# Decoder layer on one core: column scales multiplied into the float32 FFN weights, one VectorE operation per FFN row tile, and an earlier release for GpSimd

## What is computed

```python
x = layernorm(x + mamba(x))                 # conv, selective scan over 1024 x 16 states, out projection
x = layernorm(x + cross_attention(x, ctx))  # softmax(q k^T), used as x @ attention^T
x = layernorm(x + ffn(x))

def ffn(x, weight, bias):                   # int8 in effect: both sides rounded to -127..127
    w_scale = max(|weight|, axis=1) / 127   # one per output column o
    w_q = round(weight / w_scale)
    x_scale = max(|x|, axis=2) / 127        # one per row
    x_q = round(x / x_scale)
    return (x_q @ w_q.T) * x_scale * w_scale[o] + bias
```

## Time and profile before

| | us |
|---|---|
| median of 3 runs | 1086.15 (1085.72 to 4713.28) |
| the profiled execution, its own time | 1085.01 |
| its span (first to last instruction) | 1083.1 |

### The profile page before, as it was taken

The page is one execution under the profiler, slowest core; times in us unless marked ns, Lnnn a source line. Parts: engine busy times, 40 slices in busy tenths (PEclk is TensorE's granted clock), DMA queues, the critical chain, the costliest instruction groups (busy, mean ns, idle before and its releaser), DMA issues.

```text
span 1083.1 us, 10459 instructions
## 1 busy us (share of the span) xinstructions
PE 850.6 (79%) x2958; PEld 334.8 (31%) x2968; DVE 1017.7 (94%) x861; ACT 790.7 (73%) x1171; POOL 667.3 (62%) x260
## 2 busy tenths in 40 slices
PE   8945788786799899687599899887699475755985
PEld 3321233231233344232134344332133132222432
DVE  3699999999999998999999998999999999999746
ACT  4486687776766898997766898998676695876524
POOL 1056666666676766776667756786766766776343
PEclk9987798898899899999899999988799778877998
DMA  6354445453743444343743453343833532243001
GB/s 195 83 129 109 107 115 127 106 135 103 204 110 75 128 117 125 82 123 87 232 115 97 127 126 98 78 117 102 243 88 87 156 93 72 68 138 85 11 0 40
DMA packets 58474, 120.08 MB, mean 111 GB/s; under 512 B 12208, under 2 KB 18480, under 8 KB 58416
## 3 DMA queue, kind: packets, MB, share of 16 engines
q1 hardware_dynamic: 57696, 119.34, 41.9%
q10 hardware_dynamic: 720, 0.08, 0.1%
HBM read 48.07 MB, written 4.19 MB: 48 GB/s over the span
## 4 chain that ended last, share of the span: by engine, by line
DVE 32%; issue 29%; PE 19%; ACT 9%; DMA 4%; POOL 4%; SPq 2%; DVEq 0%; POOLq 0%; ACTq 0%
DVE st L768 20%; PE dense L876 12%; DVE dBu L760 7%; ACT dA L551 4%; PE dense L913 3%; POOL st L445 3%; DMA rep<-steps 2%; PE dense L944 2%; ACT L551 2%; DMA out<-x 2%; SPq L357 1%; DVE dense L859 1%; DVE xsc L824 1%; DVE x L706 1%; DVE steps L746 1%
## 5 line engine op out<-in xcount | busy, mean ns | idle before, releaser
L445 POOL TENSOR_TENSOR st<-st,Cb 128x2048 f32<-128x2048 f32 x127 | 575.1, 4528 | 368.1 <-DVE dBu L760 263.3
L768 DVE TENSOR_TENSOR_SCAN st<-dA,dBu 128x1024 f32<-128x1024 f32 x256 | 570.2, 2268 | 0.4 <-ACT dA L551 0.4
L551 ACT ACTIVATE dA<-rep,Aneg 128x511 f32<-128x511 f32 x512 | 329.2, 712 | 54.4 <-DVE st L768 49.6
L760 DVE TENSOR_TENSOR dBu<-rep,Bb 128x1024 f32<-128x1024 f32 x256 | 324.1, 1310 | 1.9 <-DMA rep<-steps 1.9
L876 PE MATMUL dense<-xTs,Win 128*128 128x512 f32 x504 | 236.4, 615 | 13.5 <-ACT wide L556 6.6
L913 PE MATMUL dense<-st,sel 128*32 128x512 f32 x1024 | 138.7, 689 | 64.5 <-POOL st L445 63.0
L876 PEld LDWEIGHTS dense<-xTs,Win 128*128 128x128 f32 x504 | 98.7, 199 | 142.8 <-issue 141.8
L876 PE MATMUL dense<-wide,hs 128*128 128x512 f32 x256 | 115.8, 605 | 6.7 <-ACT xTs L671 4.5
L944 PE MATMUL dense<-pj,Win 128*128 128x512 f32 (+1 forms) x192 | 94.8, 640 | 18.9 <-issue 18.5
L551 ACT ACT_TABLE_LOAD x75 | 96.2, 1283 | 17.4 <-DVE st L768 16.3
L913 PEld LDWEIGHTS dense<-st,sel 128*32 128x32 f32 x1024 | 33.4, 124 | 167.4 <-issue 91.2
(11 more groups left out here) (110 smaller groups left out, 733.6 us busy)
## 6 DMA issues: line engine op xcount, KB each, us to landing
rep<-steps SPq DMA_DIRECT2D x512, 128.0 KB, 2.4
Win<-w_in SPq DMA_DIRECT2D x64, 256.0 KB, 2.9
wide<-w_out SPq DMA_DIRECT2D x4, 2048.0 KB, 10.1
Win<-w_conv SPq DMA_DIRECT2D x24, 256.0 KB, 2.9
xTs<-xT SPq DMA_DIRECT2D x3, 1024.0 KB, 5.7
x<-x SPq DMA_DIRECT2D x3, 1024.0 KB, 6.0
out<-x SPq DMA_DIRECT2D x12, 256.0 KB, 2.0
wide<-w_x SPq DMA_DIRECT2D x4, 640.0 KB, 4.9
```

What stands on the lines that cost most here:

```text
L445: nc.gpsimd.tensor_tensor(s, s, Cb[:], ALU.mult).then_inc(s_p, NH)
L551: nc.scalar.activation(dA[:, u % 2, j, 1:T], rep[:, u % REPS, 0, 1:T], ACT.Exp, scale=Aneg[:, u % UNITS, j:j + 1]).then_inc(s_dA, 1)
L760: V.tensor_tensor(dBu[:, j, :], rep[:, u % REPS, 1:2, :].to_broadcast([P, JH, T]), Bb[:, j, :], ALU.mult).then_inc(s_mul, 1)
L768: V.tensor_tensor_scan(st[:, u % RING, j, :].rearrange("p j t -> p (j t)"), dA[:, u % 2, j, :].rearrange("p j t -> p (j t)"), dBu[:, j, :] ...
```

## The change

The rounded weights are multiplied by their column scales on VectorE (float32) before they are turned, so `WfT` holds float32 products of integer and scale, and `xqT` the rounded rows in float32. The FFN product is then a float32 matmul of the same shape, and its result lacks only the row scale. VectorE's operation of L859 goes: `add_rows` takes the row scale in place of 1.0. The key `ws`, its matmuls and `ws_bc` go. `sel` is 128x32, made by four `affine_select`. `xqT` now covers the place of `bc_s`, so `bc` of batches 2 and 3 waits for an `ff` (it stands behind it in every queue). `weigh_states(u)` waits for the first product of unit u+1 alone, or for both where the unit has step inputs, and not for the step inputs any more. Three tables move items to other steps. In `xsc` and `xinv` the row scales use the tiles of the column scales.

```diff
--- before.py
+++ after.py
@@ -40,14 +40,14 @@
-REST = {"wo": [2, 3, 7, 8], "q": [5], "k": [1], "en": [7, 9, 10, 11], "at": [10, 12, 14, 14],
-        "xt": [13, 13, 15, 17], "av": [15, 17, 19, 19], "qt": [17, 20, 22, 23], "ff": [19, 21, 23, 27]}
+REST = {"wo": [2, 3, 6, 7], "q": [3], "k": [1], "en": [5, 9, 10, 11], "at": [10, 12, 13, 14],
+        "xt": [13, 13, 14, 16], "av": [15, 17, 19, 19], "qt": [17, 20, 22, 23], "ff": [19, 22, 23, 25]}
 REST_BESIDE = {"q": [22], "k": [22], "en": [23, 23, 26, 27], "at": [26, 27, 28, 29], "wp": [27, 28, 29, 30]}
...
-HID_AT = [6, 9, 10, 13, 15, 17, 21, 23]
-CONV_AT = [9, 10, 13, 14, 17, 18, 22, 24]
+HID_AT = [5, 9, 10, 13, 16, 17, 19, 22]
+CONV_AT = [8, 10, 13, 14, 17, 18, 21, 24]
 DT_AT = 25
@@ -106,8 +106,6 @@
         keys += [("w", 0, 2 * (g - 1)), ("w", 0, 2 * (g - 1) + 1)]
-    if b == 0 and g == 4:
-        keys.append(("ws", 0, 0))
     if g % 4 == SUM_AT and 0 <= n - 1 < NB * NE:
@@ -154,9 +152,9 @@
         Wdt = sb("Wdt", [P, E])
-        WfT = sb("WfT", [P, KH, H], BF16)
+        WfT = sb("WfT", [P, KH, H])
         ident = sb("ident", [P, P])
-        sel = sb("sel", [P, P])
+        sel = sb("sel", [P, 32])
         Aneg = sb("Aneg", [P, UNITS, NJ])
@@ -170,7 +168,6 @@
         winv = sb("winv", [P, KH])
-        ws_bc = sb("ws_bc", [P, H])
@@ -208,8 +205,7 @@
         xq = small[:, 0:2 * T].rearrange("p (s t) -> p s t", s=2)
-        xqT = small[:, 2 * T:3 * T].bitcast(BF16).rearrange("p (s k t) -> p s k t", s=2, k=KH)
-        wide_scale = small[:, 0:KH * P].rearrange("p (k c) -> p k c", k=KH)
+        xqT = small[:, 2 * T:4 * T].rearrange("p (s k t) -> p s k t", s=2, k=KH)
         bc_s = small[:, 3 * T:4 * T]
@@ -222,8 +218,8 @@
         rsum = sb("rsum", [P, 2])
-        xsc = sb("xsc", [P, TT])
-        xinv = sb("xinv", [P, TT])
+        xsc = wscale[:]
+        xinv = winv[:]
@@ -405,7 +401,7 @@
-                        product_done(sp, ("ws", 0, 0))
+                        product_done(sp, ("w", 0, KH - 1))
                     sp.dma_start(rows_of[b], x[b].rearrange("(i p) h -> p i h", p=P)).then_inc(s_xr, 16)
@@ -428,19 +424,21 @@
-            for n, d in enumerate(range(-3, 4)):
+            for n, d in enumerate(range(-3, 1)):
                 if n:
...
                 nc.gpsimd.affine_select(out=sel[:], in_=sel[:], compare_op=ALU.not_equal, fill=1.0,
-                                        base=32 * d, pattern=[[-1, P]], channel_multiplier=1).then_inc(s_masks, 1)
+                                        base=32 * d, pattern=[[-1, 32]], channel_multiplier=1).then_inc(s_masks, 1)
             def weigh_states(u):
...
                     pool.wait_ge(s_scan, NH * (u + 1))
-                    pool.wait_ge(s_mul, NH * (u + 2))
-                    pool.wait_ge(s_du, step_inputs_before(u + 2))
+                    if step_inputs_at(u + 1):
+                        pool.wait_ge(s_mul, NH * (u + 2))
+                    else:
+                        pool.wait_ge(s_mul, NH * (u + 2) - 1)
                     s = st[:, u % RING]
@@ -477,7 +475,7 @@
-        NMASKS = 4 + 1 + 7
+        NMASKS = 4 + 1 + 4
@@ -645,12 +643,12 @@
                     elif kind == "w":
-                        integers(key, WfT[:, :, i * P:(i + 1) * P])
-                    elif kind == "ws":
-                        copied(key, ws_bc[:], lambda ps: ps)
+                        copied(key, WfT[:, :, i * P:(i + 1) * P], wide_rows)
                     elif kind == "dt":
...
                     elif kind == "bc":
+                        if kb >= 2:
+                            product_done(act, ("ff", kb - 2, TT - 1))
                         copied(key, bc_s, lambda ps: ps)
@@ -698,12 +696,12 @@
-            def add_rows(key, x_i, ps, free):
+            def add_rows(key, x_i, ps, free, scale=1.0):
...
                     normalized(dve, norm_keys[n - 4])
-                V.scalar_tensor_tensor(x_i, ps, 1.0, x_i, ALU.mult, ALU.add,
+                V.scalar_tensor_tensor(x_i, ps, scale, x_i, ALU.mult, ALU.add,
                                        accum_out=rowsum[:, n % 4:n % 4 + 1]).then_inc(free, 1)
@@ -782,12 +780,9 @@
                 for i in range(KH):
-                    rounded(x1[:, i, :], x1[:, i, :], winv[:, i:i + 1]).then_inc(s_wq, 1)
-                for i in range(KH):
-                    if i == KH - 1:
-                        dve.wait_ge(s_wq, KH)
-                    ins = V.tensor_scalar(wide_scale[:, i, :], sel[:], 0.0, wscale[:, i:i + 1], ALU.mult, ALU.add)
-                ins.then_inc(s_wq, 1)
+                    link(rounded(x1[:, i, :], x1[:, i, :], winv[:, i:i + 1]))
+                    V.tensor_scalar(x1[:, i, :], x1[:, i, :], ROUND, wscale[:, i:i + 1], ALU.subtract,
+                                    ALU.mult).then_inc(s_wq, 1)
@@ -853,12 +848,8 @@
                         ps, free = full(key)
-                        if kb == 0 and i == 0:
-                            product_read(dve, ("ws", 0, 0))
-
-                        link(V.scalar_tensor_tensor(ps, ps, xsc[:, i:i + 1], ws_bc[:], ALU.mult, ALU.mult))
                         dve.wait_ge(s_xb, TT * kb + i + 1)
-                        add_rows(key, x_i, ps, free)
+                        add_rows(key, x_i, ps, free, xsc[:, i:i + 1])
                         if kb == LAST:
@@ -980,13 +971,6 @@
                         turned(key, x1[:, i, :])
-                    elif kind == "ws":
-                        pe.wait_ge(s_wq, KH + 1)
-                        ps, done = bank_of(key)
-                        for k in range(KH):
-                            mm = nc.tensor.matmul(ps[:, k * P:(k + 1) * P], wide_scale[:, k, :], ident[:],
-                                                  start=True, stop=True)
-                        mm.then_inc(done, 1)
                     elif kind in ("wp", "wo"):
```

## The result

The change takes **1068.96 us** (median of 4 runs, 1068.53 to 1069.83), the kernel before 1085.93 us beside it: a ratio of 0.9846 (95% interval 0.9827 to 0.9865), 1.5% faster. That is the same by the bound of 2%, 4.0 us under the forecast of 1073 us, and inside its range. The profiled execution took 1068.53 us.

A forecast was written before the change was run, and what follows sets the result against it. VectorE, busy 94% of the span, was taken as the bound. Terms -19.2 - 7.9 - 0.7 + 7.2 + 4.1 + 3.4 = -13.1 us took 1085.0 to 1071.9, plus 1.1 for the median: 1073 us, range 1059 to 1087.

The forecast's parts named there:

- The port: VectorE's dBu products: GpSimd's earlier release stops leftover state products lengthening the next pair, 19.2 us gained.
- new collisions: Behind unit 54 in three batches: a late state product and a bias addition delay units 55 and 56, 4.1 us lost.
- The scaling: VectorE's 16 scalings go; 11 of them, with no later wait, give 0.72 us each, 7.9 us gained.
- TensorE in batches 1 and 2: Longer FFN products and a moved hidden projection make VectorE wait 3.6 us more in each batch, 7.2 us lost.
- The end: After the last state, four float32 FFN products fill TensorE until 1080.5 us, 3.4 us lost.
- the last state product: At the end of the last unit it finishes 0.4 us earlier, 0.4 us gained.
- The start: Four selections instead of seven before the first product: between 0 and 1.25 us gained, taken as 0.3 us.
- Batch 3: TensorE has idle time there; one scaling ahead of a 6 us wait for TensorE was counted as nothing.
- the second (the port's loss stays): State products end 4.64 to 4.76 us after the pair, 13 to 19 us missing: 1086 to 1092 us, chance 0.13.
- the third (TensorE held up by ScalarE): ScalarE, busy in batches 1 and 2, costs 3 to 6 us more per batch: 1079 to 1086 us, chance 0.1.
- The first, that TensorE holds nobody up: VectorE loses nothing to TensorE: 1066 us, or 1059 us with the old waits gone too, chance 0.2.
- The fourth (GpSimd gets in first): A state product goes ahead of VectorE's next instruction, 4.4 us each; from 8 cases 1108 us and more, chance 0.04.

The follow-up runs named there:

- e2: The kernel before with GpSimd's new wait and nothing else of the change: 1065.81 us, ratio 0.9818.
- e4: The change with both sides of the FFN product in bfloat16, the scaled weights rounded to it: 1057.51 us, ratio 0.9741.
- e1: The change with GpSimd's old wait, for both products and the step inputs: 1084.75 us, ratio 0.9987.
- e12: The change with GpSimd waiting for both products of the unit again, but not for the step inputs: 1081.22 us, ratio 0.9948.
- e7: The change with GpSimd waiting for one product everywhere, also where step inputs follow the pair: 1149.96 us, ratio 1.0566.
- e3: The kernel before without the scaling of L859, row scale in the addition, column scales not applied: 1078.27 us, ratio 0.9931.
- e11: e4 (bfloat16 FFN products) with the step tables of the kernel before: 1058.93 us, ratio 0.9749.
- e8: The change with scaled weights as a sum of two bfloat16 parts, eight matmuls for each FFN product: 1062.77 us, ratio 0.9781.
- e6: The change with the fourth FFN product of batch 2 at step 27 of batch 3, as before: 1072.11 us, ratio 0.9870.
- e9: e8 with the step tables of the kernel before, except batch 2's last FFN product kept at step 25: 1061.19 us, ratio 0.9769.
- e10: The change with the attention's own parts at their steps of the kernel before: 1069.71 us, ratio 0.9848.

## Why the prediction was right, and where it was not

The sum was -13.1 us against a measured -16.5 us of the profiled executions, and the median lay 0.4 us above its profiled run in place of 1.1.

- **The port**, -19.2 with +4.1 for new collisions: -15.1. Measured over the dBu products and step inputs: -7.9 - 3.2 - 3.2 - 1.0 = **-15.3 us**. The two halves are right too: in e2, which has the port's part alone, the dBu products come to -20.0 us (forecast -19.2), and the change has 4.7 us more than e2 on both lines (forecast 4.1). The state products end 4.37 us after the pair, as forecast. At unit 55 the collision came with 0.92 us for 0.8; the one of 0.6 us at unit 56 came in batch 3 alone (unit 120, 0.52 us), since VectorE's wait at unit 55 let the bias addition finish in batches 1 and 2 (e4 has no such wait, and has the 0.52 us there). Batch 3 has the 1.07 us of unit 121 besides, which I had not foreseen. e1 gives 15.8 us by itself. Of these 3.5 are the wait for the step inputs that GpSimd no longer passes (e12), which the prediction had only as the way of the semaphore. That VectorE's products and GpSimd's exclude each other and a running one is not slowed is what the trace shows, and what the Trainium skill says (SBUF — State Buffer, Who interferes with whom). Its sentence "Whoever issues first gets the shared pair for the whole instruction", which stands there behind VectorE's two-port modes, holds in 25 of e7's 31 units: in the 9 where VectorE issued first, and in 16 of the 22 where GpSimd did. In the other 6 GpSimd had issued first and the step inputs went ahead. The 115 ns of the same page (A bandwidth-pool intuition that's wrong), measured there on a transfer issued by GpSimd, are not seen on top of a state product: 4.37 us after the pair is less than the 4.52 us that one takes alone.
- **The scaling**, -7.9: measured -2.6 in each of three batches, -7.9 us. The prediction had 11 at 0.72 us and one that buys nothing; the timeline has 12 at 0.66 us, so two small misses cancel. The 7.9 us of e3 are another sum, as said above.
- **TensorE in batches 1 and 2**, +7.2: measured 2 x 3.9 = +7.8 us. In each of the two the waits are 1.2 us behind unit 49, 2.6 behind 50, 2.4 behind 52, 0.3 behind 53 and 0.8 behind 55, 7.3 us in all; in the kernel before there were 0.3, 0.6 and 2.6 at 45, 48 and 50. Of the 3.9 us, 0.8 come with the new wait alone (e2: VectorE is there earlier, as the sum had it), and 2.8 and 2.6 us go when the float32 products go (e4).
- **The end**, +3.4 (and -0.4 for the last state product): measured +3.4 us for both together, in place of +3.0. TensorE, against the earlier trace rows:

```profile
1045.23 3.70 PE L867 MATMUL dense<-WfT,small 128*128 128x512 f32 x8 [0.34 <-ACT small L562]
...
1049.21 3.60 PE L867 MATMUL dense<-WfT,small 128*128 128x512 f32 x8
...
1053.36 7.13 PE L867 MATMUL dense<-WfT,small 128*128 128x512 f32 x16
```

and VectorE's last addition:

```profile
1060.53 0.75 DVE L704 SCALAR_TENSOR_TENSOR hs<-dense,wscale,hs 128x512 f32<-128x512 f32 x1 [1.50 <-PE dense L867]
```

The four float32 products with two turned tiles take 1045.23 to 1060.49 us, 15.3 us in place of the 14.8 of the forecast, and TensorE ends it all. The 0.4 us of the last state product did come: it ends 6.7 us after the start of unit 127 in place of 7.1, VectorE's wait for the last state sum is 6.1 us in place of 6.5, and the end is 0.4 us shorter in the change than in e1, and in e2 than in the kernel before.
- **The start**, -0.3: measured +0.3 us. The sign is the other, but the difference can't be put down to the change. TensorE, against the earlier trace rows:

```profile
4.53 5.75 PE L922 MATMUL dense<-xTs,Win 128*128 128x512 f32 x8 [4.53 <-DMA xTs<-xT]
```

It begins 0.18 us earlier, but eight entries take 5.75 us in place of 5.24. Its entries are some 0.86 us apart up to 8.07 us and 0.43 us from 8.82 us on; in the kernel before they are 0.43 us apart from 8.07 us on. The wider spacing is that of the lower level of TensorE's clock (1.2 GHz), the closer one that of the higher (2.4 GHz): in batch 3 of the kernel before, entries are 0.85 us apart from 995.6 to 1000.8 us, with a granted clock of 0.50, and 0.43 us from 1001.4 us on, with 1.00. The profile gives 1.00 for 4.5 to 10.5 us too, but the trace has no clock record ahead of 7.9 us (8.7 us in the change), and where it has none the mean counts it as full. In all 14 kernels the first unit starts 41.2 us after this product's end. That end lies anywhere between 9.75 us (e11) and 11.05 us (e8), depending on when the clock rises. e2 and e3, whose start is that of the kernel before, begin their first unit 0.8 and 0.7 us later than it does. So beginning 0.18 us earlier neither gained nor cost anything that can be told apart here.
- **Batch 3 is the step that failed in size.** The prediction said of it that VectorE's waits stay: one scaling ahead of a wait of 6 us "I count as nothing", and for TensorE that it has idle time there. With three scalings and the port that made about -4 us, and the stage gave -8.5. The waits shrank by 4.5 us, of which e6 gives 3.1 back (and 0.7 in dBu products) for one number in a table. The diff shows that number, and the rotation of the banks was told in the text ahead; I did not follow it into batch 3. Behind the rest stands the 1.8 us that VectorE waited at the gate multiplication of unit 121, and no longer does. That wait is there in the kernels whose second FFN product is at step 21 (0.9 us in e2, 1.2 in e9, 1.6 in e11) and in none that has it at 22, e10 with the attention's old steps among them. No run moves that number alone, so this part is not shown.

Of the rivals, the second (the port's loss stays) and the third (TensorE held up by ScalarE) did not occur. The first, that TensorE holds nobody up, would have given 1059 to 1066 us. It is false for the change, whose waits for TensorE in batches 1 and 2 doubled. e4 and e8 lie near its times, at 1057.5 and 1062.8 us, but about half of what they save against the change or more comes from the end, and VectorE still waits for TensorE in e4. The fourth (GpSimd gets in first) did not occur in the change, and did in e7.

## What to carry to other kernels

Let an engine that wants a shared port be released one instruction early, so that it queues for the port behind the running instruction, but only where the instruction after that doesn't want the port: the same edit gave 15.8 us here and cost 81 us where one did. Weigh each part of a change alone: here one wait gave 20.4 us alone and the whole change 17.0 us, since float32 products on a busy TensorE cost more (11.4 us) than the operation that they saved (7.9 us). And where buffers go round in turn, an item moved in one place changes what others wait for further on; follow the rotation to the end of the list. A total that comes out near can hide a term that is missing: here the waits of one stage gave 4.5 us and had been counted as nothing.

## What the hardware showed beyond that

- A wait that is already met, behind one that isn't, delayed GpSimd's instruction by 0.06 us each time (0.23 to 0.17 us). The kernel without it is 3.5 us faster.
- An instruction of GpSimd that waits for the port behind a VectorE instruction can go next or be overtaken by VectorE's following one: 16 to 6 in one execution, 16 and 5 of them with the same moments of issue to 0.01 us. The four runs of that program differ by 14 us.
- At the start of the program TensorE's float32 entries are 0.86 us apart, the spacing of the lower clock level, and 0.43 us from a moment between 7.9 and 10.5 us on. That moment differs between kernels, those with the same start among them, and moves the first unit by up to 1.3 us. The profile's mean of 1.00 there rests on missing clock records.
- FFN products of four matmuls of 128x512 cost 3.4 to 3.6 us each in float32, and the whole kernel 11.4 us more than in bfloat16. Made of eight bfloat16 matmuls on split weights they cost 5.3 us more than bfloat16, of which 2.4 us are VectorE's subtractions.
